# Window attention: residual and join move from GpSimd to VectorE, transfers and matrix parts change places

## The reference

```
y    = layernorm(groupnorm(x))                       # the kernel reads it as yln
tok  = 16 x 16 windows of groupnorm(x), step 14      # 19 x 19 windows per image
q, k = y @ wq, y @ wk      (4 heads of 16)           # per window, 256 tokens
v    = y @ wv              (4 heads of 24)
out  = softmax(q k^T / 4) v
tok  = out @ wproj + tok
x2   = windows added where they overlap, halved per overlapping strip
xs   = x + x2                                        # kept for the end of the layer
```

## Time and profile before

| what | number |
|---|---|
| profiled execution, its own time | 7065.86 us |
| its span | 7064.1 us |
| median of the three timed runs | 7102.86 us |
| granted TensorE clock, mean of the span | 0.936 |
| attention, first to last maximum (L816) | 682.7 to 3901.4 us |
| TENSOR_REDUCE L816, VectorE | x1444, mean 1227 ns |
| STREAM_TRANSPOSE L835, VectorE | x304, mean 665 ns |
| ACTIVATE L683, ScalarE | x1444, mean 1021 ns |
| ACTIVATE L670, ScalarE | x304, mean 597 ns |
| residual L629 and L633, GpSimd (96x448) | x272 each, mean 1401 and 1124 ns |
| store of x2 (L497), 1344 KB | median 7.3 us to landing |
| ACT at_packed L670 waits for DMA at_k<-at_packed | 124.0 us, 35 times |

### The profile page before, as it was taken

One profiled execution on the slowest core, in us unless ns is written; L12 is line 12 of the kernel. 1 busy time (PEld: TensorE's weight loads), 2 busy tenths in 40 slices (PEclk: granted clock), 3 DMA queues, 4 the chain that ended last, 5 costly groups with the idle time before them and its releaser, 6 DMA issues. The chain is left out here.

```text
span 7064.1 us, 136670 instructions
## 1 busy us (share of the span) xinstructions
PE 6050.0 (86%) x51768; PEld 3121.7 (44%) x51768; DVE 4893.7 (69%) x7120; ACT 3489.9 (49%) x5182; POOL 3103.3 (44%) x4987
## 2 busy tenths in 40 slices
PE   0885999999999999999999589989997766588885
PEld 0332555555555555555555233335554111076661
DVE  7796777777777777777777355558886545556664
ACT  0553666666666666666666356644443111154340
POOL 0443677777776777777776656610000000000000
PEclk9997999999999999999999799999999888799995
DMA  7685344444444444444443598788897999636665
GB/s 306 195 242 162 72 99 105 102 102 105 105 105 95 101 101 99 99 103 99 99 95 71 129 273 238 233 289 343 345 345 261 297 306 309 205 103 201 190 187 180
DMA packets 761672, 1252.70 MB, mean 177 GB/s; under 512 B 159364, under 2 KB 477828, under 8 KB 730948
## 3 DMA queue, kind: packets, MB, share of 16 engines
q1 hardware_dynamic: 700532, 1090.77, 55.3%
q10 hardware_dynamic: 53328, 102.85, 4.9%
q0 software_dynamic: 7168, 50.34, 2.1%
HBM read 680.81 MB, written 508.40 MB: 168 GB/s over the span
## 5 line engine op out<-in xcount | busy, mean ns | idle before, releaser
L816 DVE TENSOR_REDUCE at_mz<-at_ps 128x4 bf16<-128x1024 f32 x1444 | 1771.2, 1227 | 557.5 <-PE at_ps L735 550.1
L683 ACT ACTIVATE at_E<-at_ps 128x1024 f32<-128x1024 f32 x1444 | 1399.4, 1021 | 387.0 <-PE at_ps L747 368.6
L747 PE MATMUL at_ps<-at_qaug,at_k 32*128 32x256 f32 x11552 | 847.0, 408 | 26.6 <-DVE at_qaug L843 26.6
L758 PE MATMUL at_ps<-at_E,at_vaug 128*32 128x256 f32 x11552 | 782.5, 388 | 5.3
L1282 PE MATMUL cv_ps<-cv_yin,cv_band 128*128 128x384 f32 x2304 | 746.4, 486 | 26.2 <-DMA cv_yin<-y_mlp 26.2
L747 PEld LDWEIGHTS at_ps<-at_qaug,at_k 32*128 32x128 f32 x11552 | 532.1, 188 | 509.8 <-issue 350.1
L1302 DVE TENSOR_TENSOR cv_yin<-cv_gl,cv_yin 64x384 f32<-64x384 f32 x1152 | 637.4, 553 | 150.4 <-ACT cv_gl L1293 142.6
L1564 POOL MEMSET cs_eps<- 96x1 f32 x1 | 0.1, 95 | 1500.5 <-POOLq L1312 1500.5
L735 PE MATMUL at_ps<-at_k,at_q 32*128 32x256 bf16 x5776 | 578.0, 276 | 9.0 <-DMA at_k<-at_packed 7.5
L1282 PEld LDWEIGHTS cv_ps<-cv_yin,cv_band 128*128 128x128 f32 x2304 | 436.7, 190 | 336.2 <-DMA cv_yin<-y_mlp 27.1
L1293 ACT ACTIVATE cv_gl<-cv_ps,cv_bias 128x384 f32<-128x384 f32 x576 | 334.4, 581 | 437.4 <-PE cv_ps L1282 437.4
(11 more groups left out here) (217 smaller groups left out, 10351.0 us busy)
## 6 DMA issues: line engine op xcount, KB each, us to landing
cv_yin<-y_mlp SPq DMA_DIRECT2D x48, 2340.0 KB, 14.8
s_mlp<-cv_yin SPq DMA_DIRECT2D x48, 2340.0 KB, 8.4
at_rows_in<-y_attention SPq DMA_DIRECT2D x76, 768.0 KB, 6.2
gn_xin<-in_x SPq DMA_DIRECT2D x16, 3072.0 KB, 23.2
ln_xin<-in_x SPq DMA_DIRECT2D x192, 256.0 KB, 7.3
y_attention<-ln_xin SPq DMA_DIRECT2D x192, 256.0 KB, 3.8
cl_xu<-x SPq DMA_DIRECT2D x128, 384.0 KB, 3.7
cl_xv<-x SPq DMA_DIRECT2D x64, 768.0 KB, 6.3
```

Source lines behind the costliest of these rows:

```text
L683: act.activation(E[:, m % 2, 2 * p:2 * p + 2, :], psum[:, 2 + 2 * p:4 + 2 * p, :], ACT.Exp).then_inc(exp_done, 1)
L747: i = pe.matmul(psum[:, 2 + h, TOK * j:TOK * j + TOK], k[rows, n % 2, tokens(w, 128 * j, 128)], qaug[rows, m % 2, :], start=True, stop=True)
L758: i = pe.matmul(pv_ps[32 * h:32 * h + VC, 0:TOK], vaug[:, m % 2, z, h, :], E[:, m % 2, h, z * TOK:(z + 1) * TOK], start=(z == 0), stop=(z ...
L816: dve.tensor_reduce(mz[:, m % 2].rearrange("p j (h c) -> p h j c", c=32)[:, 2 * p:2 * p + 2, :, DQ], psum[:, 0:2, :].rearrange("p h (j n) ...
```

## The change

The residual (as one instruction) and the join go to VectorE, behind the turned result and ahead of the second maximum; turning back goes there too, in windows 0 to 7. `saved` has two buffers. Projections stand in windows 1 to 8, queries and keys in 9 to 16, residuals in 9 to 16, `both` in 10 to 17. On TensorE the parts follow the second half of the first scores; on ScalarE their copies stand between the two exponentials. On SyncE the store of x2 goes behind all four `spread_heads`, the load for the band after next ahead of them.

```diff
-    QK_AT = 8
-    END = NW + YP
+    PROJ_AT, QK_AT, RES_AT, BOTH_AT = 1, 9, 9, 10
+    END = NW + PROJ_AT + YP
...
-        saved = sb("saved", [128, CC, STEP])
-        xscaled = sb("xscaled", [C, PS, CC])
+        saved = sb("saved", [128, 2, CC, STEP])
...
+        def proj_at(n):
+            nb, w = where(n)
+            return (nb - 1, w - PROJ_AT) if 1 <= nb <= NB and PROJ_AT <= w < PROJ_AT + YP else None
+        def residual_at(n):
+            nb, w = where(n)
+            first = RES_AT if nb < NB else PROJ_AT + 1
+            return (nb - 1, w - first) if 1 <= nb <= NB and first <= w < first + YP else None
...
@@ sync
                 if more:
                     load_y(n + 1, 1)
-                if n:
-                    store_x2(n - 1)
+                if n + 2 < NB:
+                    load_y(n + 2, 0)
                 if more:
                     spread_heads(n + 1, 0)
                     spread_heads(n + 1, 1)
                 if n:
                     store_xs(n - 1, 0)
-                if n + 2 < NB:
-                    load_y(n + 2, 0)
...
                 if more:
                     spread_heads(n + 1, 3)
                 if n:
+                    store_x2(n - 1)
                     store_xs(n - 1, 1)
@@ gpsimd
-                if whole(n - 5):
-                    join(*whole(n - 5))
+                if back_at(n + 1):
+                    save(*back_at(n + 1))
                 if 0 <= n - 3 < NW:
                     normalise(n - 3)
-                if whole(n - 3):
-                    save(*whole(n - 3))
                 if nb + 1 < NB and w < 4:
                     turn_columns(nb + 1, w)
-                if nb + 1 < NB and 9 <= w < 13:
-                    turn_columns(nb + 1, w - 5)
-                if nb >= 1 and 1 <= w < 1 + YP:
-                    residual(nb - 1, w - 1)
+                if nb + 1 < NB and 6 <= w < 10:
+                    turn_columns(nb + 1, w - 2)
+                if both_at(n):
+                    both(*both_at(n))
@@ scalar
             for n in range(END):
+                if 0 <= n - 1 < NW:
+                    exponential(n - 1, 0)
                 if qk_at(n):
                     queries_and_keys(*qk_at(n))
                 if proj_at(n):
                     projected(*proj_at(n))
                 if 0 <= n - 1 < NW:
-                    exponential(n - 1, 0)
                     exponential(n - 1, 1)
                     values(n - 1)
@@ tensor
                 if n < NW:
                     scores_for_max(n, 0)
+                if 0 <= n - 1 < NW:
+                    scores(n - 1)
+                if n < NW:
+                    scores_for_max(n, 1)
                 if qk_at(n):
...
                     projected += 1
-                if 0 <= n - 1 < NW:
-                    scores(n - 1)
-                if n < NW:
-                    scores_for_max(n, 1)
@@ vector
+                if rows:
+                    dve.wait_ge(ot_done, YP * n + c + 1)
+                    a = ot[:, cols(c), 0:rows]
+                    dve.tensor_tensor(a, a, saved[:, c % 2, :, 0:rows], ALU.add).then_inc(joined, 1)
+
+            def residual(n, c):
+                rows = own_rows(n)
+                dve.wait_ge(pr_out, YP * n + c + 1)
+                if c % 4 == 0:
+                    dve.wait_ge(x_loaded[c // 4], 16 * (n + 1))
+                a = xa[:, 0:rows, cols(c)]
+                dve.scalar_tensor_tensor(out=a, in0=xr[:, 0:rows, cols(c)], scalar=t["gn_scale"][:, n // NWIN:n // NWIN + 1], in1=a,
+                                         op0=ALU.mult, op1=ALU.add).then_inc(x2_done, 1)
...
                 if 0 <= n - 3 < NW:
                     turn(n - 3)
+                if back_at(n):
+                    turn_back(*back_at(n))
+                if residual_at(n):
+                    residual(*residual_at(n))
                 if n < NW:
                     maxima(n, 1)
                 if 0 <= n - 3 < NW:
                     denominators(n - 3)
-                if whole(n - 4):
-                    turn_back(*whole(n - 4))
```

More of the change, by code:

```diff
@@ L419, in attention @@
             sem(s) for s in ("max_done", "qaug_done", "turned_done", "rden_done", "ot_done"))
-        share_done, weighted, heads_done, saved_done, joined, scaled = (
-            sem(s) for s in ("share_done", "weighted", "heads_done", "saved_done", "joined", "scaled"))
+        share_done, weighted, heads_done, saved_done, joined = (
+            sem(s) for s in ("share_done", "weighted", "heads_done", "saved_done", "joined"))
         x_loaded = [sem(f"x_loaded{i}") for i in range(2)]
@@ L469, in qk_at, with back_at, both_at @@
             return (nb + 1, w - QK_AT) if n < NW and nb + 1 < NB and QK_AT <= w < QK_AT + YP else None
-        def whole(n):
+        def back_at(n):
             nb, w = where(n)
-            return (nb, WHOLE_AT.index(w)) if 0 <= n < NW and w in WHOLE_AT else None
+            return (nb - 1, w) if 1 <= nb <= NB and w < YP else None
         def proj_at(n):
             nb, w = where(n)
-            return (nb - 1, w) if 1 <= nb <= NB and w < YP else None
+            return (nb - 1, w - PROJ_AT) if 1 <= nb <= NB and PROJ_AT <= w < PROJ_AT + YP else None
[3 more added lines that the diff above has]
+            return (nb - 1, w - first) if 1 <= nb <= NB and first <= w < first + YP else None
+        def both_at(n):
+            nb, w = where(n)
+            return (nb - 1, w - BOTH_AT) if 1 <= nb < NB and BOTH_AT <= w < BOTH_AT + YP else None
         @block.sync
@@ L606, in save @@
                 if rows:
-                    if n % NWIN == 1:
+                    if shared_rows(n - 1):
+                        pool.wait_ge(joined, joins(n - 1, c))
+                    else:
                         pool.wait_ge(ot_done, YP * (n - 1) + c + 1)
[L609 to L633, removed]
+                    if joins(n, c) > 2:
+                        pool.wait_ge(joined, joins(n, c) - 2)
+                    pool.tensor_copy(saved[:, c % 2, :, 0:rows], ot[:, cols(c), PS - rows:PS]).then_inc(saved_done, 1)
             def both(n, c):
@@ L642, in _ @@
                 turn_columns(0, piece)
-            for n in range(END + 1):
+            for n in range(END):
                 nb, w = where(n)
-                if whole(n - 5):
-                    join(*whole(n - 5))
+                if back_at(n + 1):
+                    save(*back_at(n + 1))
                 if 0 <= n - 3 < NW:
                     normalise(n - 3)
-                if whole(n - 3):
-                    save(*whole(n - 3))
                 if nb + 1 < NB and w < 4:
                     turn_columns(nb + 1, w)
-                if nb + 1 < NB and 9 <= w < 13:
-                    turn_columns(nb + 1, w - 5)
-                if nb >= 1 and 1 <= w < 1 + YP:
-                    residual(nb - 1, w - 1)
-                if nb >= 1 and nb < NB and 9 <= w < 9 + YP:
-                    both(nb - 1, w - 9)
+                if nb + 1 < NB and 6 <= w < 10:
+                    turn_columns(nb + 1, w - 2)
+                if both_at(n):
+                    both(*both_at(n))
             for c in range(YP):
@@ L829, in turn_back @@
             def turn_back(n, c):
+                rows = shared_rows(n)
                 dve.wait_ge(heads_done, NWIN * n + WHOLE_AT[c] + 1)
-                if shared_rows(n):
+                if rows:
                     dve.wait_ge(saved_done, joins(n, c))
@@ L848, in _ @@
             dve.wait_ge(filled, 6)
-            for n in range(NW + 4):
+            for n in range(END + 1):
                 if n < NW:
```

## The result

The changed kernel takes 7292.95 us (median of four runs, 7285.56 to 7300.04) against 7102.08: ratio 1.0272, interval 1.0254 to 1.029, some 191 us slower. The prediction was 7273 in 7190 to 7375. The profiled execution of after has 7288.81 us.

What follows compares the result with a forecast made beforehand. TensorE was taken as the bound in windows with a part, within a ring with VectorE's first maximum. Terms 107 + 160 + 2 + 18 - 103 - 14 = +170 us on 7103 gave 7273 us, range 7190 to 7375.

Steps and rivals of the forecast that it cites:

- queries and keys behind L735: Queries-and-keys windows: the part moved behind TensorE's second first scores (L735) makes 4.84 us of 4.48, +107 us over 296 windows.
- projections behind L735: Projection windows: the part behind TensorE's second first scores (L735) makes 4.92 us of 4.35, +160 us over 280 windows.
- windows with a small projection: Windows of the two bands whose projection has 64 columns, at 3.90 already: 16 x 0.1 = +2 us.
- window 0: First window of a band, now without a part: VectorE's turning back is exposed, 4.40 us against 3.90, +18 us.
- stall: ScalarE's wait at part 4 for copies out of `packed`, slowed by the store of x2: all goes, -103 us.
- tail: Attention's end: each addition follows its own residual on VectorE, so the stage ends sooner, -14 us (bounds 0 and -20).
- The ring: Bare window: VectorE's first maximum, then TensorE from L735 to the next L735; work behind L735 lengthens it one for one.
- TensorE stays full: Rival: parts behind L735 cost what they do now, -99 us, 7004 us; chance 0.10 together with rival (4).
- The projection's copy: Projection windows: ScalarE's copy (1.04 us) must free the PSUM bank before L765, adding 0.21 us: 4.92.
- rival (4): The move to VectorE is the gain, the order neutral, GpSimd never waited for in the bands; 0.10 with "TensorE stays full".
- margin of 0.7 us: Last eight copies out of `packed`: landing at 11.5 us from window 16's start, needed by window 0 at 12.2.
- my upper bound: VectorE's residual in the bands: at most 2.04 ns an element beside GpSimd, 0.92 us; 0.8 taken.

Runs made afterwards that it cites:

- the order alone: The kernel before with nothing but the new order of the parts on TensorE and ScalarE: 7286.11 us, ratio 1.0275.
- half the copy: The changed kernel with ScalarE copying only 16 of 32 columns of every projection: 7217.64 us (one run).
- the run with the order put back: The changed kernel with the parts on TensorE and ScalarE ordered as before the change, everything else kept: 6992.88 us, ratio 0.9861.

## Why the prediction was right

The sum was +170. The measured terms are all windows of a kind, added up in the two traces:

| term | predicted | measured |
|---|---|---|
| queries and keys behind L735 | +107 | +107 (296 windows, 4.85 each) |
| projections behind L735 | +160 | +184 (280 windows, 5.01 - 4.35 = 0.66 each) |
| windows with a small projection | +2 | +6 |
| window 0 | +18 | +15 (37 x 0.39) |
| stall (windows 12 and 13 over 4.48) | -103 | -104 |
| tail | -14 | -8 |
| sum | +170 | +200 (trace 199.6) |

**The ring** is shown: 4.84 forecast, 4.85 measured; the order alone gives +194 us, net of the stall that goes with it, and putting it back brings the windows with a part to where they were. The rival "TensorE stays full" fell in the same two runs, and with it the one that put the gain into the move to VectorE. One of the signs I had named fell short: TensorE is below 95% busy in the projection windows (91%), but not in those with queries and keys (37.30 of 38.78, 96%).

**The projection's copy** was undersized. I let L765 start 0.06 us behind the copy and the copy last 1.04; it lasted 1.08 and L751 started 0.14 behind its end. The window came to 5.01, not 4.92: 0.09 x 280 = 25 us of the 30 that the sum is short of the trace. With half the copy the window is at 4.71, my figure for TensorE alone, so nothing else is in that term.

**Window 0** was named, but not windows 1 to 7 of the two bands with a small projection, which stand at 4.29 too.

**The stall** went, and by what I had priced, but my reason covers half of it. I put it on the slow issues behind the store. The first copies also stood 4.2 us behind that store, and the store behind GpSimd's last residual. So the prediction was wrong where it said that GpSimd matters nothing in the bands, and its rival (4) that GpSimd "was never waited for": SyncE waited for it, and in 35 of the 36 bands from 1 to 36 that held released copies for 3.5 us or more. That the new order of the parts would end the stall by itself, as the order alone shows, I had not seen. I had also feared for the last copies, with a margin of 0.7 us: released in window 16, they landed 6.7 us later in band 14, not 8.1, 2.1 us ahead of their need, and no window waited for them. The run with the store ahead of them shows that 3 us more would have been too many.

**The tail** gave 8 us, not 14 (41.4 us from the last maximum's start to the stage's end in place of 49.7; that last maximum starts at 3903.2 in the kernel before, not at 3901.4). From the timeline, not tried: beside GpSimd's last additions the residual takes 1.74 us in place of 0.74, and both last stores are issued within 1.4 us.

**The offset.** I kept the 37 us between profile and median. The profiled execution of after lies 4 us from its median. Outside attention, where all kernels here are the same, the profiled execution of before takes 3793.9 us, and those of the other ten kernels 3809.4 to 3829.6. Their median is 3819, so some 25 of the 37 us belong to one quick execution, in stages that the change leaves alone, and keeping them was right, though I had no reason for it but that nothing said they would go. In its own terms the sum is 30 us short (170 of 200); that the forecast lies only 20 us from the measured median (7273 and 7293) is in part luck, since the medians differ by 191 and the attention of the two traces by 200.

## What to carry to other kernels

Find the ring before moving work: an engine that is busy all the time may still have its idle time filled by the very piece that is to be moved. Here a part ahead of the scores cost 0.45 to 0.58 us a window and behind them 0.95 to 1.11, though TensorE did the same matmuls. When several edits come together, run each half alone: here one half lost 194 us and the other, with the old order, won 99. A queue that issues in order ties engines together that share no data: here a copy of ScalarE's output stood behind a store that stood behind GpSimd, and so GpSimd, for which the compute engines hardly waited, had its part in a stall of ScalarE. And take away a wait only together with what is next: the store moved last alone took 101 us out of two windows and gave back 32 in others.

## What the runs showed of the hardware

VectorE's instruction with two SBUF inputs can lose more to GpSimd than I had bounded. The same residual (96x512) in the tail of the changed kernel:

```profile
4138.44 1.74 DVE L835 SCALAR_TENSOR_TENSOR at_xa<-at_xr,t_gn_scale,at_xa 96x512 f32<-96x512 f32 x1
...
4147.95 0.75 DVE L835 SCALAR_TENSOR_TENSOR at_xa<-at_xr,t_gn_scale,at_xa 96x512 f32<-96x512 f32 x1 [1.61 <-ACT at_xa L676]
```

The first runs beside GpSimd's additions, the second while GpSimd is idle: a factor of 2.3, or 3.4 ns an element where my upper bound was 2.04. A rate by the element is the wrong measure, though: the added time goes with the overlap. In the run with the order put back, a GpSimd instruction (its addition L628 or a copy) overlaps each 96x448 residual by some 0.4 us, and the residual's median is 0.88, against 0.64 with no overlap in the changed kernel:

```profile
L834 DVE SCALAR_TENSOR_TENSOR at_xa<-at_xr,t_gn_scale,at_xa x304: 239/880/1745, 805.2 to 3848.1; 96x448 f32<-96x448 f32 x136, 96x64 f32<-96x64 f32 x8, 96x512 f32<-96x512 f32 x8
```

In the run with the residual done twice, an overlap of 0.41 us added 0.25 and one of 0.52 added 0.36 to 0.95. The Trainium skill (GPSIMD Engine Reference, Specifications) names this contention without a size. In the bands of the changed kernel it did no harm, because the residual begins (at 1.50) behind GpSimd's addition (to 1.16).

A large store ahead of small copies slows their issue on SyncE: four copies of 64 KB took 5.53, 5.88 and 6.30 us behind the store of 1344 KB, in three kernels, and 2.40 to 2.42 without it.
